# A fused convolutional mixer and mixture-of-experts block: first-layer weights loaded in another order, small statistics moved to GpSimd, steps laid out anew

## The reference

```
x = x + mixer(layernorm over channels(x))
t = tokens of x                                   # 4096 tokens of 64 channels
t = t + moe(layernorm(t))

mixer(u): z, xBC, dt = split(W_in u)              # 128, 160, 8 channels
          dt  = softplus(dt + dt_bias)
          xBC = silu(depthwise 3x3 conv(xBC) + conv_b);  xs, B, C = split(xBC)
          KV  = sum over pixels of B * (xs * dt * exp(A_log))
          y   = (C KV + xs * D) * silu(z)
          out = W_out (layernorm(y) * ln_g + ln_b)
moe(t):   top 2 of 8 softmax gates;  sum over experts of gate_e * (gelu(t W1_e + b1_e) W2_e + b2_e)
```

## Time and profile before

| | |
|---|---|
| median of 3 runs | 160.89 us (160.42 to 161.43) |
| the profiled execution's own time | 161.06 us |
| its span, first to last instruction | 158.8 us |
| mean granted TensorE clock | 0.993 |
| TensorE busy | 143.4 us (90%) |
| VectorE busy | 112.3 us (71%) |
| ScalarE busy | 93.8 us (59%) |
| GpSimd busy | 80.4 us (51%) |

### The profile page before, as it was taken

One profiled execution on the slowest core, in us unless ns is written; L12 is line 12 of the kernel. 1 busy time (PEld: TensorE's weight loads), 2 busy tenths in 40 slices (PEclk: granted clock), 3 DMA queues, 4 the chain that ended last, 5 costly groups with the idle time before them and its releaser, 6 DMA issues.

```text
span 158.8 us, 3263 instructions
## 1 busy us (share of the span) xinstructions
PE 143.4 (90%) x1106; PEld 57.3 (36%) x1106; DVE 112.3 (71%) x294; ACT 93.8 (59%) x178; POOL 80.4 (51%) x149
## 2 busy tenths in 40 slices
PE   6889998999999997999999998989879979999950
PEld 1244435563454554343435442224322222222210
DVE  1396977999888885889997889993566952353540
ACT  2265477436883587785689648645547638485430
POOL 7600750484018005647524945535959335779870
PEclk9999999999999999999999999999999999999997
DMA  4910600000000008930001991201990207940022
GB/s 106 193 16 12 172 30 0 4 4 2 0 0 4 0 8 206 244 83 2 0 0 34 246 233 32 66 0 46 252 231 15 66 12 191 228 111 0 0 66 70
DMA packets 9658, 11.87 MB, mean 75 GB/s; under 512 B 4130, under 2 KB 7594, under 8 KB 9642
## 3 DMA queue, kind: packets, MB, share of 16 engines
q1 hardware_dynamic: 8394, 10.94, 29.5%
q10 hardware_dynamic: 1248, 0.72, 2.0%
HBM read 10.48 MB, written 1.18 MB: 73 GB/s over the span
## 4 chain that ended last, share of the span: by engine, by line
PE 64%; DVE 21%; issue 5%; ACT 3%; DMA 3%; SPq 1%; DVEq 0%; ACTq 0%
PE pm L1060 14%; PE pe L1165 8%; PE pe L1180 8%; PE pe L1060 5%; PE pm L1180 5%; PE pm L1165 5%; DVE tmp L939 4%; DMA cw_x<-in_L_conv_conv_w_dram 3%; PE pr L1124 2%; PE pm L1070 2%; PE pr L1110 2%; DVE x L903 2%; PE pm L1078 2%; DVE g L874 1%; DVE xo L898 1%
## 5 line engine op out<-in xcount | busy, mean ns | idle before, releaser
L472 POOL TENSOR_TENSOR acc<-acc,tmp 128x256 f32<-128x256 f32 x54 | 38.3, 733 | 21.7 <-DVE tmp L939 20.9
L636 ACT ACTIVATE hid<-pe,b1T 128x512 f32<-128x512 f32 x48 | 30.2, 681 | 10.5 <-PE pe L1165 10.4
L1165 PE MATMUL pe<-fst,w 64*128 64x512 f32 x96 | 26.5, 627 | 1.4 <-ACT hid L636 1.4
L1180 PE MATMUL pe<-hid,w 128*32 128x512 f32 x192 | 25.5, 601 | 0.9 <-DVE tmp L939 0.6
L939 DVE SCALAR_TENSOR_TENSOR tmp<-pe,b2T,gates 128x512 f32<-128x512 f32 x24 | 17.9, 745 | 10.6 <-PE pe L1180 10.6
L1060 PE MATMUL pm<-pad,wT 64*128 64x512 f32 x108 | 25.1, 600 | 0.0
L663 DVE SCALAR_TENSOR_TENSOR bcc<-bcp,cw_bc,bcc 128x256 f32<-128x256 f32 x32 | 15.5, 483 | 0.9
L636 ACT ACTIVATE hid<-pm,b1T 128x512 f32<-128x512 f32 x16 | 10.1, 684 | 8.7 <-PE pm L1165 6.3
L1060 PEld LDWEIGHTS pm<-pad,wT 64*128 64x128 f32 x108 | 9.9, 185 | 11.9 <-issue 11.9
L417 POOL TENSOR_TENSOR r<-ve,halves 128x8 f32<-128x8 f32 x3 | 5.0, 1676 | 17.7 <-DVE ve L784 17.7
L1165 PEld LDWEIGHTS pe<-fst,w 64*128 64x128 f32 x96 | 7.8, 185 | 15.1 <-issue 15.0
(11 more groups left out here) (220 smaller groups left out, 231.1 us busy)
## 6 DMA issues: line engine op xcount, KB each, us to landing
gates<-cwd SPq DMA_DIRECT2D x32, 256.0 KB, 5.7
xin<-in_x_dram SPq DMA_DIRECT2D x6, 128.0 KB, 3.4
out_dram<-acc SPq DMA_DIRECT2D x6, 128.0 KB, 2.5
w<-in_L_ffn_W_dram SPq DMA_DIRECT2D x2, 256.0 KB, 4.9
xin<-in_x_dram ACTq DMA_DIRECT2D x2, 128.0 KB, 4.2
w<-in_L_ffn_W_dram ACTq DMA_DIRECT2D x1, 256.0 KB, 4.4
cwd<-cwS SPq DMA_DIRECT2D x4, 32.0 KB
out_dram<-acc SPq DMA_DIRECT2D x2, 64.0 KB, 2.3
```

The lines of the kernel that those rows point to most:

```text
L472: ins = pool.tensor_tensor(acc[p][:, half], (x2 if e == 0 else acc)[p][:, half], tmp[ln][e % 2][:, half], ALU.add)
L636: act.activation(hid[ln][e % 2][:, q, :], expert_banks(g)[q][:], ACT.Gelu, bias=b1T[:, e:e + 1]).then_inc(hid_in[ln].sem, 1)
L1165: ins = pe.matmul(expert_banks(g)[q][:], w1[half, place(e, q), :], fst[p][half, :], start=True, stop=True)
L1180: ins = pe.matmul(bank[C * q + c:C * q + c + BC, half], w2[:, e, c:c + BC], hid[ln][e % 2][:, q, half], start=True, stop=True)
```

## The change

- **Loads.** SyncE's order was: first half of image group 0, z half of W_in, cw_x, W1's first half, the B, C and dt rows of W_in (`wbd_raw`), first half of group 1. Now it is: first half of group 0, cw_x, wbd_raw, z half, both halves of group 1, W1's first half. ScalarE no longer issues the second half of group 1.
- **Taps.** `twc` is split: `twx` centres the x half when it is there, `twz` the z half. `tpa` (taps 0 to 3) becomes four ScalarE instructions of 128x128 with a scale; `tpb` (taps 4 to 8) stays on VectorE.
- **Variances.** The three 128x8 instructions move from VectorE to GpSimd, ahead of the power, for all three norms, except group 0 of the first norm. VectorE keeps the transpose.
- **dt.** `dt1` and `dtv` become `dtp` on GpSimd, four instructions of 128x64; the absolute value is now 2 max(v, 0) - v. Group 0's transpose stays on VectorE as a step of its own, `dtT`.
- **Order.** `PLAN` is new. At the start `sm1` comes before `cv00` and `wa0` after `rb0`; `nT0` and `ne0` come earlier; `u10` stands ahead of `sm3`; in the last stage the experts of groups 2 and 3 are interleaved a little differently.

```diff
-busy0 busy0 busy0 busy0 busy0 busy0 sq0 sx0 twc0 sm0 busy0 busy0 busy0 ve0 busy0 busy0 tb0 wa0 sr0 tpa0 tw0 rw0
-tTa0 ta0 ini0 tpb0 rb0 wbe0 dt0 xn0 tea0 tTb0 sq1 dt10 cv00 dtv0 ex0 teb0 sf00 ea0 sm1 wae0 bd0 tec0 ve1 cv10
-bcp0 k00 pw1 k10 sf10 rx1 cv20 nm0 k20 rb1 xs00 z0 xs10 sf20 xn1 bcs0 xt00 sz00 dt11 v00 sz10 xt10 bt0 v10 bd1
-btc0 dtv1 sq2 kv0 bcp1 nT0 kvc0 sq3 k01 sm2 ne0 y0 ve2 cv01 ex1 y00 pw2 sf01 rx2 cv11 gs00 y10 sf11 k11 gs10 rb2
-c00 xn2 ps0 cf0 k21 bd2 cv21 bcp2 gst0 sf21 pwg0 k02 pj0 xs01 rxg0 dt12 z1 k12 xs11 rbg0 pc0 dtv2 cv02 bcs1 x20
...
+busy0 busy0 busy0 busy0 busy0 busy0 busy0 sq0 sx0 twx0 sm0 tpa0 busy0 tb0 busy0 twz0 tw0 tTa0 ta0 tpb0 busy0
+busy0 tea0 ve0 tTb0 sq1 ini0 sm1 sr0 teb0 rw0 dt0 dtT0 rb0 ve1 dtp0 wa0 xn0 tec0 cv00 pw1 ex0 ea0 sf00 wbe0 wae0
+bd0 dtp1 rx1 cv10 bcp0 k00 sf10 ex1 k10 cv20 nm0 k20 rb1 xs00 sf20 xs10 z0 xn1 bcs0 xt00 sz00 nT0 v00 sz10 xt10
+ne0 bt0 v10 bd1 btc0 sq2 kv0 bcp1 c00 kvc0 sf01 cf0 sm2 y0 ve2 cv01 pw2 y00 k01 sf11 rx2 cv11 y10 gs00 k11 gs10
+sq3 rb2 ps0 xn2 pj0 gst0 k21 pwg0 bd2 pc0 cv21 bcp2 bcs1 k02 dtp2 rxg0 sf21 rbg0 xs01 cv02 x20 k12 ex2 sq20 s20
...
             load(0, (0,))
-            sp.dma_start(wxz_raw[:, 1], twice(W_in[0:DI, :])).then_inc(d_proj, 16)
-            sp.dma_start(cw_x[:], cw_v[0:DI, :]).then_inc(d_proj, 16)
+            sp.dma_start(cw_x[:], cw_v[0:DI, :]).then_inc(d_cwx, 16)
+            sp.dma_start(wbd_raw[:], twice(W_in[2 * DI:2 * DI + BC + NH, :])).then_inc(d_wbd, 16)
+            sp.dma_start(wxz_raw[:, 1], twice(W_in[0:DI, :])).then_inc(d_z, 16)
+            load(1)
             sp.dma_start(w1[0:C, :, :], W1.rearrange("e c f -> c e f")).then_inc(d_w1, 16)
-            sp.dma_start(wbd_raw[:], twice(W_in[2 * DI:2 * DI + BC + NH, :])).then_inc(d_wbd, 16)
-            load(1, (0,))
...
+        def variance(engine, c, at, stats, squares, var, out, eps):
+            mean, mean_sq = stats
+            engine.tensor_tensor(squares[:], mean, mean, ALU.mult).then_inc(c.sem, 1)
+            engine.wait_ge(c.sem, at + 1)
+            engine.tensor_tensor(var[:], mean_sq, squares[:], ALU.subtract).then_inc(c.sem, 1)
+            engine.wait_ge(c.sem, at + 2)
+            engine.tensor_scalar(out, var[:].rearrange("p j q -> p (j q)"), 0.0, eps, ALU.max, ALU.add).then_inc(c.sem, 1)
...
                 if step == "pw":
...
-                    pool.wait_ge(var_eps.sem, var_eps.at(g, 4))
+                    pool.wait_ge(turned.sem, turned.at(g, 1))
+                    variance(pool, var_eps, var_eps.at(g, 0), (t1[p][:, 0, :, 0:2], t1[p][:, 1, :, 0:2]), mq[p], vv[p],
+                             ve[p][:], 1e-6)
+                    pool.wait_ge(var_eps.sem, var_eps.at(g, 3))
                     pool.tensor_tensor(r1[p][:], ve[p][:], halves[:], ALU.pow).then_inc(rstd.sem, 1)
+                elif step == "dtp":
...
+                    pool.wait_ge(rstd.sem, rstd.at(g, 1))
+                    pool.tensor_tensor(dtv[p][:].rearrange("p (j q) h -> p j q h", q=2),
+                                       t1[p][:, 0, :, 2:2 + 2 * NH].rearrange("p j (q h) -> p j q h", h=NH),
+                                       r1[p][:].rearrange("p (j q) -> p j q", q=2).unsqueeze(3)
+                                       .broadcast_to([P, TJ, 2, NH]), ALU.mult).then_inc(c.sem, 1)
+                    pool.wait_ge(c.sem, c.at(g, 1))
+                    pool.tensor_tensor(dtv[p][:], dtv[p][:], dtb[:].unsqueeze(1).broadcast_to([P, NT, NH]),
+                                       ALU.add).then_inc(c.sem, 1)
+                    pool.wait_ge(c.sem, c.at(g, 2))
+                    pool.tensor_scalar(dtm[p][:], dtv[p][:], 0.0, 2.0, ALU.max, ALU.mult).then_inc(c.sem, 1)
+                    pool.wait_ge(c.sem, c.at(g, 3))
+                    pool.tensor_tensor(dta[p][:], dtm[p][:], dtv[p][:], ALU.subtract).then_inc(c.sem, 1)
...
+                elif step == "tpa":
+                    act.wait_ge(i_tap, 2)
+                    act.wait_ge(d_cwx, 16)
+                    for t in range(4):
+                        act.activation(taps[:, t, :], wxz[:, 0].rearrange("p r c -> p (r c)"), ACT.Copy,
+                                       scale=cw_x[:, t:t + 1]).then_inc(i_tpa, 1)
...
-                    if g == 0:
-                        act.dma_start(xin[1][C:2 * C, :].rearrange("c (b l) -> c b l", b=2), x_v[1, 1]).then_inc(d_x[1], 16)
```

More of the change, by code:

```diff
@@ L24 @@
[L24 to L33, removed]
@@ new lines @@
+bd0 dtp1 rx1 cv10 bcp0 k00 sf10 ex1 k10 cv20 nm0 k20 rb1 xs00 sf20 xs10 z0 xn1 bcs0 xt00 sz00 nT0 v00 sz10 xt10
+ne0 bt0 v10 bd1 btc0 sq2 kv0 bcp1 c00 kvc0 sf01 cf0 sm2 y0 ve2 cv01 pw2 y00 k01 sf11 rx2 cv11 y10 gs00 k11 gs10
+sq3 rb2 ps0 xn2 pj0 gst0 k21 pwg0 bd2 pc0 cv21 bcp2 bcs1 k02 dtp2 rxg0 sf21 rbg0 xs01 cv02 x20 k12 ex2 sq20 s20
+z1 ve20 k22 pw20 xs11 cv12 sz01 sf02 sz11 bcs2 sf12 rt00 xt01 bt1 xt11 v01 th0 cv22 rx20 rt10 btc1 v11 rb20 xs02
+rt20 kv1 xs12 z2 kvc1 xn20 y1 sz02 sf22 sz12 cwt0 xt02 y01 cwc0 bt2 xt12 gw0 btc2 v02 u00 v12 h00 y11 kv2 gs01
@@ new lines @@
+u10 kvc2 gs11 sm3 h10 y2 ve3 pw3 ps1 y02 d00 gst1 pj1 m00 pwg1 rx3 u20 y12 gs02 pc1 rb3 d10 xn3 a00 rxg1 bd3
+gs12 m10 rbg1 bcp3 dtp3 h20 cv03 x21 k03 sq21 s21 d20 ve21 ex3 k13 pw21 u30 cv13 sf03 h30 sf13 rt01 rx21 u40 k23
+th1 cv23 h40 rt11 a10 u50 m20 xs03 rt21 a20 rb21 xs13 z3 bcs3 sf23 d30 xn21 sz03 sz13 xt03 m30 cwt1 bt3 xt13
+cwc1 v03 a30 btc3 gw1 ps2 d40 gst2 v13 h50 pwg2 pj2 m40 kv3 pc2 d50 kvc3 a40 rxg2 u60 m50 rbg2 h60 a50 y3 x22
+u70 y03 sq22 d60 h70 s22 ve22 gs03 u01 m60 pw22 y13 h01 d70 u11 m70 a60 rx22 rt02 d01 h11 a70 rb22 m01 gs13 u21
@@ new lines @@
+th2 xn22 a01 st0 d11 h21 rt12 pj3 m11 u31 pc3 rt22 a11 d21 h31 cwt2 m21 cwc2 u41 gw2 a21 ps3 h41 d31 gst3 pwg3
+u51 m31 d41 h51 m41 a31 rxg3 u61 rbg3 h61 a41 d51 x23 u71 m51 sq23 h71 s23 a51 d61 ve23 u02 pw23 m61 d71 h02 m71
+u12 a61 rx23 rt03 rb23 h12 d02 a71 xn23 th3 u22 m02 st1 rt13 u03 a02 h22 d12 h03 rt23 u32 m12 cwt3 d03 cwc3 h32
+gw3 a12 d22 u13 m22 u42 a22 h13 d32 h42 u23 m32 u52 a32 h23 d42 h52 u33 m03 u62 m42 a03 d13 h62 d52 m13 a42 h33
+d23 m52 a13 u43 m23 u72 h43 a52 d33 h72 a23 u53 m33 d43 h53 a33 d62 m43 u63 a43 m62 d53 h63 a62 d72 m53 u73 a53
@@ L37 @@
+m72 d63 h73 a72 m63 d73 a63 st2 m73 a73 st3
 """.split()
@@ L157, in metaformer_block @@
         dtv = two("dtv", [P, NT, NH])
+        dtm = two("dtm", [P, NT, NH])
         dta = two("dta", [P, NT, NH])
@@ L173, in metaformer_block @@
         gv = two("gv", [P, TJ, 2])
+        gw_ = two("gw_", [P, TJ, 2])
         ge = two("ge", [P, TJ, 2])
@@ L742, in steps @@
                                              scalar=-1.0 / C, in1=wbd_raw[:], op0=ALU.mult, op1=ALU.add).then_inc(i_dve, 1)
[L743 to L753 removed]
+                elif step in ("twx", "twz"):
+                    n = int(step == "twz")
+                    c = (i_tap, i_twz)[n]
+                    dve.wait_ge((d_proj, d_z)[n], 16)
+                    dve.reduce_sum(wxz_sum[:, 2 * n:2 * n + 2], wxz_raw[:, n], axis=AX.X).then_inc(c, 1)
+                    dve.wait_ge(c, 1)
+                    dve.scalar_tensor_tensor(out=wxz[:, n], in0=wxz_sum[:, 2 * n:2 * n + 2].unsqueeze(2)
+                                             .broadcast_to([P, 2, C]), scalar=-1.0 / C, in1=wxz_raw[:, n],
+                                             op0=ALU.mult, op1=ALU.add).then_inc(c, 1)
+                elif step == "tpb":
+                    n = TAPS - 4
                     dve.wait_ge(i_tap, 2)
[L755 removed]
+                    dve.wait_ge(d_cwx, 16)
+                    dve.tensor_tensor(taps[:, 4:TAPS], wxz[:, 0].rearrange("p r c -> p (r c)").unsqueeze(1)
                                       .broadcast_to([P, n, 2 * C]),
[L757 removed]
+                                      cw_x[:, 4:TAPS].unsqueeze(2).broadcast_to([P, n, 2 * C]),
+                                      ALU.mult).then_inc(i_tap, 1)
                 elif step == "tec":
@@ L883, in steps @@
                     dve.wait_ge(stat.sem, stat.at(g, 1))
[L885 to L892 removed]
+                    dve.transpose(tg[p][:].rearrange("p j r -> p (j r)"), pr[1][:, 0:P]).then_inc(o_turned.sem, 1)
                 elif step == "x2":
@@ L905, in steps @@
                 elif step == "ve2":
[L906 removed]
                     if g > 1:
                         dve.wait_ge(rstd2.sem, rstd2.at(g - 2, 1))
+                        dve.wait_ge(rt.sem, rt.at(g - 2, 1))
                     dve.wait_ge(stat2.sem, stat2.at(g, 1))
[L911 to L919 removed]
+                    dve.transpose(t2[p][:].rearrange("p m j r -> p (m j r)"), pr[0][:, 0:2 * P]).then_inc(turned2.sem, 1)
                 elif step == "xn2":
@@ L966, in steps @@
                     pe.wait_ge(i_pool, 2)
-                    pe.wait_ge(i_tap, 3 if step == "tTa" else 4)
+                    if step == "tTa":
+                        pe.wait_ge(i_tpa, 4)
+                    else:
+                        pe.wait_ge(i_tap, 3)
+                        pe.wait_ge(i_twz, 2)
                     for n in part:
```

144 lines of the change are left out of this document (50 added, 94 removed).

## The result

The changed kernel took 161.44 us in the median of 20 runs (160.75 to 162.54), the kernel before 160.79 in as many. The ratio is 1.0049, 95% interval 1.0034 to 1.0064: slower by 0.8 us (the medians differ by 0.65), where 1.9 us less were forecast. The prediction held that a change under 1% can't be told from none; twenty runs of each tell this 0.5% from none. The profiled execution after took 160.99 us for a span of 159.1. That alone would say "no change" against the 161.06 of before. But from the last matmul to the end of the span it shows 4.3 us, before's 4.9, and thirteen of the seventeen profiles of this study show 4.3 (the others 4.7 to 5.1). Where I place a gain or a loss, I compare the start of the same TensorE step in two profiles; how large it is, I take from the timed ratios.

The account below looks back on a forecast made before the run. TensorE, busy 143.4 of 158.8 us, was taken as the bound, so only its 15.4 us idle could be won. Terms -0.5 - 0.6 - 0.2 - 0.8 + 0.2 = -1.9 gave 159.0 us, range 156.3 to 163.0.

Parts of the forecast that it names:

- the moved work counted at 0: Variances and dt on GpSimd: each statistic's chain 0.4 us longer but covered by other TensorE work, so 0.
- rival B: VectorE and GpSimd block each other, VectorE loses its relief again; 160.0 us, within 1%, chance 0.13.
- The cover: TensorE work ahead of the norm rows hides the longer chains: 4.2 against 3.8 us at rbg0, over 2 at rb20.
- Rival A: Statistic chains become the bound, rbg0 first, if a small GpSimd step takes over 0.47 us; 163.5 us, chance 0.18.
- The start: Opening up to the first convolution: cv00 at 11.5 instead of 12.02 us, -0.5, and sm1 out of the way, -0.6.
- sm1's part: sm1, 0.57 us, leaves its place between cv00 and bd0 and runs in the loading time: -0.6 us.
- The root's: First norm at the start: square root possible at 8.8 us, 0.4 later than before, yet rw0 and xn0 0.4 earlier.
- rival C: The start wins nothing, as twz0 or sq1 hold the norm or late W1 holds wa0; 160.0 us, chance 0.19.
- The relief: About 10 us of work off VectorE shortens TensorE's waits: -0.2 at kv and -0.8 in 90 to 130 us.
- kv's wait of 1.1: TensorE's wait for kv, caused by gst1 ahead of kvc2 on VectorE; 0.2 us of it was counted as gained.
- The +0.2 for one more mode change: TensorE changes between 128-row and 64-row steps 36 times instead of 35, each about 0.2 us: +0.2.
- Rival D: TensorE's waits in 60 to 130 us, 5.6 in all, are mostly VectorE's and two thirds go; 156.0 us, chance 0.14.

Follow-up runs that it names:

- e1: The changed kernel with the old order from bd0 on, variances and dt still on GpSimd; ratio to the kernel before 0.9999.
- e5: The kernel before with only the change's loads, split taps and opening order, variances and dt on VectorE; ratio to before 0.9961.
- e12: The changed kernel with three VectorE convolution steps beside sequence 1's second-norm variance cut to one image row; one execution, 161.35 us.
- e6: The changed kernel with all variances back on VectorE, new order and dt on GpSimd kept; ratio to before 0.9931.
- e13: The changed kernel with only the four output-norm variances back on VectorE; ratio to before 1.0041.
- e4: The changed kernel with one token moved, sequence 1's normalised copy xn21 (fst) ahead of rt21 on VectorE; ratio to before 0.9985.
- e3: The changed kernel in its new order, with variances and dt back on VectorE; ratio to before 0.9988.
- e10: The changed kernel with variances back on VectorE, e4's order and e8's start, dt still on GpSimd; 158.72 us, ratio to before 0.9873.
- e11: The kernel before's order with the repaired start of e8, variances and dt on VectorE; ratio to before 0.9918.
- e2: The changed kernel with the old order after its opening, variances and dt back on VectorE, dtp0 ahead of xn0; ratio to before 1.0058.
- e14: The changed kernel with only the four second-norm variances, ahead of the router, back on VectorE; ratio to before 0.9986.
- e8: e4 with the z half of W_in issued on ScalarE's queue ahead of W1 and the opening steps reordered; ratio to before 0.9971.
- e7: e6 with e4's order, so the changed kernel with variances on VectorE and xn21 ahead of rt21; ratio to before 0.9933.

## Why the prediction was wrong

**The step that failed** is the moved work counted at 0: "A statistic's chain gets 3 x 0.33 - 3 x 0.20 = 0.4 longer", and covered. In the new order the variances cost 1.9 us (1.0049 against 0.9931; by the intervals 1.4 to 2.4; by the medians 1.5); in the old order all the moved work costs 0.6 (e1 against e5). Two things were off.

The price. I took one pitch of 0.33 for all. Alone it is 0.30 in the mean of the three (e12), beside the convolution 0.42, 0.54 and 0.60, 0.52 in the mean (the chain from 72.09 to 73.65), so this chain with its handover is 0.8 longer than in e6 and 1.0 longer than before (3.30, 2.51, 2.34), not 0.4. Eight of the eleven chains have a pitch of 0.30, and the mean of all is 0.36, near enough to my 0.33; two of the three others stand ahead of a router. I had both ends (0.17 and 0.66) and rival B's row of an add at 0.32 and 0.73, but used it for VectorE's losses only, not for the small steps of GpSimd that I was pricing. It is the new order that lays the convolution's rows there: it has "gst0 k21", "ve20 k22" and "ve21 ex3 k13", where the old one has "gst0 sf21", "ve20 btc1" and "ve21 cv03".

The cover. I looked for it where TensorE waits (rbg0, rb20), and not where VectorE waits: rt stands in VectorE's queue behind the power of the same norm, and 0.97 us of idling there is then followed by 28 steps in a row to fst. For rb20 I wrote "over 2 us" of cover, which holds for TensorE's step, not for the router's. The router stood in the old order too (e1, 1.23 us); what differed was that fst came early there.

**Rival A** (0.18) had the mechanism and the threshold, 0.47, and the sign. At rbg0 the pitch was 0.51 and TensorE waited 0.43, as it said. At the other four places that it named the pitch was 0.30 and TensorE didn't wait, and the price was wrong: 1.9 us, half of it at the second norm's chains ahead of the router, not 4.0 at the five rbg and rb steps; e13 shows rbg0's wait worth 0.1.

**The start**: forecast -1.1, measured -0.44 at cv10, and -0.6 alone (e5). sm1's part came (0.43 of 0.57). The root's did not: the z half landed at 7.0 and not at 6.4 (issued at 2.87 for 2.7, in flight for 4.13 and not 3.7), and 0.6 later than forecast, at 9.38 for 8.8, the root started. This is rival C's mechanism. (From the half's issue to its sum it took 3.9 in e4 and 4.6 in e12, so one profile gives this to some tenths.) W1 was no problem, its half took 4.4 and not 5.1, and wa0 took 1.1 on the path, for 1.2 foretold.

**The relief**: forecast -1.0, measured 0 in the change (4.57 idle from 90 to 130, 4.4 before). VectorE's removed steps were busy for 9.5 us before, and its total fell by 6.5. Seven kinds of router steps grew from 9.1 us in all to 11.3. That looks like rival B, but it is the order: with all the work back on VectorE the new order has 11.3 too (e3), and the old order has 9.6 with all the work on GpSimd (e1). One of the seven groups, before, in the change and in e3 (xcount, busy us, mean ns, idle):

```profile
L691 DVE SCALAR_TENSOR_TENSOR k<-ld,rank 128x64 f32<-128x64 f32 x4 | 1.3, 334 | 0.1
```

```profile
L739 DVE SCALAR_TENSOR_TENSOR k<-ld,rank 128x64 f32<-128x64 f32 x4 | 1.9, 470 | 0.1
```

```profile
L709 DVE SCALAR_TENSOR_TENSOR k<-ld,rank 128x64 f32<-128x64 f32 x4 | 1.8, 438 | 0.1
```

With the variances back, new order and dt's move give some 0.7 us (e10 against e11). That is near the 1.0 that I had for relief, but by luck: the new order gives 1.1 with nothing taken off VectorE (e2 to e3). That relief by itself is worth anything in this kernel, no run shows.

**The sum by the runs**: start alone -0.6 (e5), order and dt's move some -0.5 (e6 less e5), variances +1.9: +0.8. This adds up to the measured result by construction, each term being the difference of two runs in a row; it says where the time went, and tests nothing. The terms hold in this succession only, since the variances' price depends on the order. Of the 1.9, 1.0 is the second norm's (e14), 0.1 the output norm's (e13); the remaining 0.8, the first norm's or what only all together give, was not run alone and stays open. Profiles place less than the timing shows: at the last down step e6 is 0.9 ahead of the change, timed 1.9, or 1.5 by the medians. The profiled executions explain part of it, e6's being 0.2 above its median and the change's 0.45 below; a single profile of this kernel is good to half a microsecond.

**Right**: GpSimd's busy time, what is removed from VectorE, the x half, sm1's part, wa0's length and the harmless end. kv's wait of 1.1 went whole where I had counted 0.2, and by the order, not by relief: it is gone in e3 and still 0.8 in e1. The +0.2 for one more mode change was not tried by itself. Rival D's two thirds of 5.6 are 3.7, not 4.0; nothing hangs on it.

## What to carry to other kernels

Before moving small steps to a less busy engine, follow the chain they belong to up to the in-order queue that waits for its end, and not only up to TensorE: here VectorE stood 0.97 us for work taken off it. Price the steps by rows in which the neighbour of their new place is running. Don't try a new order and moved work as two independent gains: here the same order was worth +1.1 us or -0.8, by where the small steps ran. And when a split load is to bring a start forward, the later half decides if anything stands behind it in the same queue; e8 moved one issue and reordered the queue, which gained 0.7 to 1.0 us at cv00, and 1.0 us timed (e10 against e7).

## What the runs showed of the hardware that I had not expected

GpSimd's 128x8 steps take 0.20, 0.20 and 0.26 us alone and 0.34, 0.45 and 0.52 beside VectorE's convolution steps (two inputs from SBUF), which keep their own 0.49. Beside g's second step, with both inputs from SBUF, the third of them took 0.74 (e1). Beside VectorE's tmp and first g step, with one input from PSUM, they stay at 0.20, 0.20 and 0.25 (95.56 in the change). VectorE does the same three in 0.17 each. The power on 128x8 took 1.66 in most places, and 1.83 in e6 (72.19) where it started beside a convolution step. A 64 KB half of W_in, fourth in SyncE's queue, took 4.13 us to land; issued 0.74 us earlier on ScalarE's queue ahead of W1's 256 KB it was summed 3.6 after its issue (e8), 4.0 in e10 and 4.5 in e11.
